# Four graph layers: counting the sources under layer 0's scatters, with the zeroing and the loads moved

## The reference, cut to what matters

```python
deg_n = segment_sum(ones, src); deg_e = segment_sum(ones, dst)
he  = Binv * segment_sum(x[src], dst)       # rows of edges into hyperedges (dst < 10000)
out = Dinv * segment_sum(he[dst], src) + b  # hyperedges back to the nodes
...
x = x + hconv(relu(hconv(h, W1)), W2)
```

## Time and profile before

| | us |
|---|---|
| median of 3 runs (3129.03 to 3147.51) | 3143.76 |
| the profiled execution | 3136.22 |
| its span | 3134.4 |

### The profile page before, as it was taken

How to read it: one execution, slowest core, us unless ns; L and a number is a source line. 1 busy time by engine, 2 the same in 40 slices (tenths; PEclk the granted TensorE clock), 3 DMA queues, 4 the chain that set the end, 5 groups by cost and what they waited for, 6 DMA issues and landing times. The chain is left out here.

```text
span 3134.4 us, 48304 instructions
## 1 busy us (share of the span) xinstructions
PE 2077.7 (66%) x10165; PEld 1475.8 (47%) x10165; DVE 2139.2 (68%) x8782; ACT 1682.8 (54%) x4590; POOL 1582.2 (50%) x1489
## 2 busy tenths in 40 slices
PE   3673534637767778788745788777776666664665
PEld 1332512525545656666632334343335655564555
DVE  5798523338877888898857777777745544444999
ACT  2592101238874656565647988898965444442222
POOL 3200565520007888888827666655607777774000
PEclk9896767879996677666767999999998888877999
DMA  2497422449997787787747999999966555554998
GB/s 72 146 360 304 80 56 75 101 114 323 322 306 264 243 249 230 244 255 234 235 103 216 290 290 286 283 294 286 292 170 216 178 186 181 181 175 137 316 316 280
DMA packets 494677, 696.59 MB, mean 222 GB/s; under 512 B 66363, under 2 KB 357398, under 8 KB 485932
## 3 DMA queue, kind: packets, MB, share of 16 engines
q1 hardware_dynamic: 416414, 511.30, 51.5%
q0 software_dynamic: 63360, 130.75, 15.6%
q10 hardware_dynamic: 14736, 52.96, 4.7%
HBM read 394.91 MB, written 327.18 MB: 230 GB/s over the span
## 5 line engine op out<-in xcount | busy, mean ns | idle before, releaser
L274 POOL DMA_INDIRECT xs<-x_d,table_src x400 | 386.7, 967 | 350.1 <-DVE x L1502 128.4
L274 POOL DMA_INDIRECT xs<-n_d,srcI x200 | 240.1, 1201 | 325.6 <-DVEq L1151 270.4
L274 POOL DMA_INDIRECT xd<-n_d,dstI x200 | 235.4, 1177 | 60.9 <-issue 54.5
L274 POOL DMA_INDIRECT xd<-x_d,table_dst x200 | 211.4, 1057 | 65.1 <-issue 64.5
L1860 PE MATMUL bank<-xs,same 128*128 128x129 f32 x400 | 109.2, 363 | 180.7 <-ACT sums L1829 93.0
L1721 POOL DMA_INDIRECT r_d<-rd,out_row x200 | 196.5, 982 | 60.9 <-issue 60.9
L1657 PEld LDWEIGHTS bank<-nmsg,same 128*128 128x128 f32 x400 | 61.4, 193 | 267.7 <-ACT sums L1589 209.0
L1657 PE MATMUL bank<-nmsg,same 128*128 128x128 f32 x400 | 99.9, 333 | 130.2 <-ACT sums L1589 74.9
L269 ACT ACTIVATE root<-tmp,eps 128x4 f32<-128x4 f32 (+3 forms) x253 | 76.8, 303 | 196.4 <-DVE tmp L245 195.8
L250 DVE RECIPROCAL rs<-root 128x4 f32<-128x4 f32 (+3 forms) x253 | 51.9, 205 | 185.5 <-ACT root L269 173.2
L474 POOL DMA_INDIRECT sum_d<-add,to x40 | 62.5, 1563 | 228.4 <-ACT add L663 187.7
(11 more groups left out here) (393 smaller groups left out, 7131.5 us busy)
## 6 DMA issues: line engine op xcount, KB each, us to landing
n_d<-T SPq DMA_DIRECT2D x98, 528.0 KB, 3.8
nt<-n_d SPq DMA_DIRECT2D x49, 1056.0 KB, 7.3
r<-r_d SPq DMA_DIRECT2D x98, 520.0 KB, 5.5
bc<-dst_d SPq DMA_DIRECT2D x170, 256.0 KB, 4.6
r_d<-nv SPq DMA_DIRECT2D x49, 528.0 KB, 7.7
v_d<-nv SPq DMA_DIRECT2D x49, 528.0 KB, 7.7
nv<-v_d SPq DMA_DIRECT2D x49, 528.0 KB, 4.3
x_d<-x SPq DMA_DIRECT2D x100, 256.0 KB, 4.8
```

Of the source, the lines that this page charges most:

```text
L274: pool.indirect_dma_start(out=out, out_offset=None, in_=table, in_offset=bass.IndirectOffsetOnAxis(ap=index, axis=0)).then_inc(s, 16)
```

## The change

The 52 source steps are placed differently: one in each group of the first gathers as before (now without the destinations, and behind the statistics), four in each group of the first scatters, and the rest, at least two, behind them. The destinations get steps of their own: three in each group of the second gathers, two in each of the second scatters, at least two behind. `hot` and `lows` shrink. `finalize` is cut in two: the source part (with a first store of `meta`) ends the first scatters, the destination part (with a second store) ends layer 0; parts of the other tables are made later too. The zeros come from padding rows of x within DRAM, 16 copies of 1.62 MB by ScalarE's queue right after the first loads. The loads are cut: 8 in `first_plan`, `K0` and ten and nine others by SyncE, ten by ScalarE; only the first 8 are waited for ahead of the columns. The two first gathers are issued ahead of the count of groups.

```diff
-            plan = [(rows...), ...]                     # 38 loads, all by SyncE
+            first_plan = [src, dst, next_dst, K, edge_weight, three columns of before]   # 8
+            plan = [...]                                # the other 29, and K0 by itself
+                    for dst, src in first_plan:
+                        sp.dma_start(dst, src, ...).then_inc(first_loads, 16)
+                    sp.dma_start(K0[:, :], ...).then_inc(k0_in, 16)
+                    for dst, src in plan[10:20]:
+                        sp.dma_start(dst, src, ...).then_inc(loads, 16)
                     sp.wait_ge(columns_in, 1)
                     for k, table in ((0, src_d), (1, dst_d)):
                         sp.dma_start(table..., rowsF[:, k, :, :]).then_inc(rows_out, 16)
+                    for dst, src in plan[20:]:
+                        sp.dma_start(dst, src, ...).then_inc(loads, 16)
...
+                    for dst, src in plan[0:10]:
+                        act.dma_start(dst, src, ...).then_inc(loads, 16)
+                    act.wait_ge(first_loads, 16 * len(first_plan))
+                    for k in range(16):
+                        act.dma_start(sum1_d[k * ZERO:(k + 1) * ZERO, :].rearrange("(p r) f -> p (r f)", p=96),
+                                      t["x"][N:N + ZERO, :].rearrange("(p r) f -> p (r f)", p=96)).then_inc(zeroed, 16)
                     act.wait_ge(weights_ps, 1)
...
-                            for k in range(NN // (P * 28)):
-                                sp.dma_start(sum1_d[...], zero_rows[:, 0:28 * D]).then_inc(zeroed, 16)
...
                     pe.wait_ge(columns_in, 1)
...
+                    pe.wait_ge(loads, 16 * len(plan))
+                    nc.tensor.transpose(bank[4][:, 0:D], wq[:, :], ident)
...
+                    def sources(k, b, of_low=False):        # TensorE
+                        pe.wait_ge(hot_ready, k + 1)
+                        pe.wait_ge(lows_ready, k + 1)
+                        for j in range(G): ...              # bank 0, of_low also bank 1
+                        last.then_inc(hot_used, 1)
+                    def destinations(k, b): ...             # bank 2, col_ready and col_used
...
                             last.then_inc(e["sums_ps"], 1)
+                            if conv == 1:
+                                for k in range(3):
+                                    destinations(g * 3 + k, (s + k) % 2)
                         bounded(pe, n, sums)
-                            bounded_from(pe, n, NH, histogram)
...
                             last.then_inc(e["he_ps"], 1)    # end of hyperedges
+                            if conv == 0:
+                                sources(n + g * 4, 0)
...
+                        def counted(g, s):
+                            for k in range(3 - conv):
+                                if conv == 0: sources(n + g * 4 + (k + 1), (k + 1) % 2)
+                                else:         destinations(n * 3 + g * 2 + k, k)
+                        lagged_thirds(pe, n, hyperedges, combined, counted)
+                        combined(n - 1, 1)
+                        m = steps_behind(pe)
+                        bounded(pe, m, behind)
...
+                            lagged_thirds(act, n, rows_of_edges, additions, signed)   # conv 0
+                            bounded(act, m, behind)
+                            additions(n - 1, 1)
...
+                            if conv == 0:                   # VectorE, reached, behind combine and later
+                                sources(n + g * 4, 0, n + g * 4)
                             dve.wait_ge(e["he_ps"], g + 3)
...                                                         # binv
+                            for k in range(3 - conv): ...   # sources or destinations
                             if conv == 0:
                                 dve.wait_ge(e["landed"], g + 1)
...                                                         # to
+                        bounded(dve, m, behind)
+                        of_sources(m) if conv == 0 else of_destinations(m)
...
+def lagged_thirds(eng, count, first, second, third):
+    first(0, 0); third(0, 0); first(1, 1); second(0, 0); third(1, 1)
+    with eng.Fori(2, count - 1, 2) as i:
+        first(i, 0); second(i - 1, 1); third(i, 0)
+        first(i + 1, 1); second(i, 0); third(i + 1, 1)
```

More of the change, by code:

```diff
@@ L43 @@
 COPY = 4096
+ZERO = 3168
 TW = 132
@@ L122, in lagged @@
     second(count - 1, 1)
+def lagged_thirds(eng, count, first, second, third):
+    first(0, 0)
+    third(0, 0)
+    first(1, 1)
+    second(0, 0)
+    third(1, 1)
+    with eng.Fori(2, count - 1, 2) as i:
+        first(i, 0)
+        second(i - 1, 1)
+        third(i, 0)
+        first(i + 1, 1)
+        second(i, 0)
+        third(i + 1, 1)
 def lagged_by_two(eng, count, first, second):
@@ L344, in build @@
                 "combine_ready", "comb_ps", "later_link", "to_ready", "add_ready", "added", "landed", "last_cols_ready",
-                "last_ps", "last_in")} for conv in range(2)]
+                "last_ps", "last_in", "counted")} for conv in range(2)]
             er_in, bc_in, sums_out, sums_back, bcd_in, bcs_in = (
@@ new lines, in sources @@
+                    def sources(k, b, at, of_low=False):
+                        dve.wait_ge(hot_used, k + 1)
+                        for j in range(G):
+                            for part, hi in enumerate(("hs", "hl") if of_low else ("hs",)):
+                                last = nc.vector.tensor_scalar(hot[:, b, j, part * NHI:(part + 1) * NHI], iota[:, 0:NHI],
+                                                               split[hi][:, bass.ds(at * G + j, 1)], None, ALU.is_equal)
+                        last.then_inc(hot_ready, 1)
@@ new lines, in destinations @@
+                    def destinations(k, b):
+                        dve.wait_ge(col_used, k + 1)
+                        for j in range(G):
+                            at = bass.ds(k * G + j, 1)
+                            nc.vector.tensor_scalar(hot[:, b, j, 0:NHI], iota[:, 0:NHI], split["hd"][:, at], None, ALU.is_equal)
+                            last = nc.vector.tensor_scalar(lows[:, b, j, :], iota[:, :], split["ld"][:, at], None, ALU.is_equal)
+                        last.then_inc(col_ready, 1)
@@ L928, in reached @@
                             nc.vector.reciprocal(binv[:, s, :], binv[:, s, :]).then_inc(e["binv_ready"], 1)
+                            for k in range(3 - conv):
+                                if conv == 0:
+                                    sources(n + g * 4 + (k + 1), (k + 1) % 2, n + g * 4 + (k + 1))
+                                else:
+                                    destinations(n * 3 + g * 2 + k, k)
                             if conv == 0:
```

324 lines of the change are left out of this document (186 added, 138 removed).

## The result

| | kernel before | changed kernel |
|---|---|---|
| median, us (range, 4 runs each) | 3145.29 (3129.03 to 3147.51) | 3198.15 (3196.93 to 3203.28) |
| profiled span, us | 3134.4 | 3196.0 |
| mean granted TensorE clock | 0.833 | 0.825 |

The ratio is 1.0184, 95% interval 1.0153 to 1.0215: slower, by 1.8%. The forecast was 3192 us. (The kernel before has one run more here than ahead of the prediction, so its median is 3145.29 and not 3143.76.) The span is read in three pieces. Up to the second gathers (`ix` on GpSimd) the changed kernel loses 33.8 us (448.12 against 414.32); from there to the start of the next block 31.4 us (287.0 against 255.6); the rest of the program is 3.6 us shorter. Sum 61.6, the difference of the spans.

A forecast was written before the change was run, and what follows sets the result against it. ScalarE's sign tables pace layer 0's counting, over full DMA engines. +38.5 us up to the second gathers and +12 after, on 3136.2, make 3187; 7.5 more for the median gives 3194, written 3192. Range 3065 to 3230.

The forecast's parts named there:

- Turns: Start of layer 0: queues alternate packet for packet, so loads wait out the zeroing and land at 104 us instead of 22.
- split of a turn: Zeroing time: 60 us for its bytes at 431 GB/s plus 48 shared turns at 0.66 us, 32 us; 88 taken.
- the low end of 60 us: Zeroing in layer 0: lowest time considered, 25.95 MB at the unshared 431 GB/s; the high end was 92.
- Rival A: Start of layer 0: a turn is many small packets, so loads land by 22 us; 3035 us in all, chance 0.2.
- First gathers: First gathers of layer 0: 6.65 us a group, the copy of x issued at 178.6 us instead of 136.4.
- Copy of x: Between first gathers and scatters: 89 us with nothing covering it, first combine at about 267 us, where it was 294.83.
- First scatters: First scatters with four counting steps a group: 16.2 us a group, 158 us for the stage, up 59.
- the ring: First scatters: additions, signs, counting, hyperedges and combined sums wait for each other in a circle, 16.2 us a group.
- Rival B: First scatters: contention as forecast, but ScalarE's 11.9 us a group sets the pace; 3152 us in all, chance 0.22.
- Behind them: From the last `to` of the first scatters to the second gathers: 27.8 us, 20.3 before.
- Second gathers and scatters: Added destination steps mostly hide under GpSimd's 11 us a group: +12 us, ends 0 and +27.
- 2.5 + 1.7 + 5.5 + 1 + 1.7: Second gathers: time of a group if the third destination step, waiting for TensorE's sums, closes late: 12.4 us.

The follow-up runs named there:

- e1: Changed kernel with the zeroing copies cut into 3 KB pieces instead of some 50 KB: 3457.41 us, one run, beside 3425.73 for the kernel before on that chip.
- e2: Changed kernel with the zeroing issued only once all loads have landed: 3487.93 us, one run, beside 3425.73 for the kernel before on that chip.
- e3: Changed kernel with the copy of x in 26 copies spread over the first scatters: 3402.18 us, one run, beside 3425.73 for the kernel before.
- e4: Changed kernel without the 40 source steps in the first scatters: 3425.85 us, one run, beside 3425.73 for the kernel before on that chip.
- e7: Changed kernel, first scatters with four table buffers, signs after the additions, counting one group late: 3501.69 us, one run, beside 3468.28 for the kernel before.
- e9: Changed kernel with e3's spread copy, e7's late count and a third destination buffer in the second gathers: 3085.93 us, ratio 0.9844 to the kernel before.
- e8: e9 with the zeroing behind all loads, partly spread over the first gathers, and smaller pieces in both copies: 3032.17 us, ratio 0.9668 to the kernel before.

## Why the prediction was right, and where it was off

The mechanism and nearly every landmark were right.

- **Turns.** First loads in and zeroing issued at 8.79 us (forecast 9). Packets one for one. Loads in with the end of the zeroing: first weight copy 100.57, h of group 0 ready at 109.8 (forecast 114.5). e1 shows that it is turns: smaller packets, same bytes, loads 53 us sooner. Not foreseen was that SyncE itself is held while it issues: 60.7 us at five 64 KB loads, 6.75 to 14.50 each, where e2, with no zeroing in the way, has 0.43 or 0.44 each. The loads came in with the end of the zeroing as forecast, so no cost of its own shows here; the same effect on ScalarE ate e1's gain. The forecast's split of a turn, the bytes at 431 GB/s and 0.66 us for the sharing, is not borne out: e1's zeroing alone ran at 332 GB/s. Its 88 us came close all the same, since it took the two parts together, which is the shared rate; the low end of 60 us rests on the 431 alone, which the copies within DRAM reach in no stretch shown here. Rival A, small loads passing the zeroing, is refuted.
- **First gathers.** 6.6 us a group, forecast 6.65; copy of x issued at 174.58, forecast 178.6.
- **Copy of x.** First combine 263.29, forecast 267. e3 shows that this stretch was bare: 74.5 us come back once the copy has cover.
- **First scatters.** 16.1 us a group, forecast 16.2; last `to` at 420.7, forecast 425. e4 and e7 show the ring. Rival B, ScalarE's 11.9 us, did not happen in the change; e7 makes it happen, at 11.7, by its order of work.
- **Behind them.** 27.4 us to the second gathers, forecast 27.8 (the terms written there, 8.5, 12.1 and 6.5, make 27.1). Up to there +33.8 against +38.5.
- **Second gathers and scatters: the mis-sized term.** +12 was forecast, with ends of 0 and +27; +31.4 was measured, beyond the high end. One of the forecast's own signs fails with it: the second gathers were to stay GpSimd's, and they are paced by the ring. The chain "2.5 + 1.7 + 5.5 + 1 + 1.7" was the right ring, but the sums were taken at 5.5 or 3.7 us where they take 5.4 in the first group and up to 6.7 in the later ones, and only 0.7 us a group was booked, where the chain with 5.5 already stands 1.4 over the 11 of GpSimd. With 6.5 the same chain gives 13.4, and the groups take 12.6 to 13.8, 13.4 in the mean, 2.3 over the 11.07 before, +20.6 in nine. e9 confirms it: with a third buffer 11.5 us. The rest, about 10 us, lies between the last h and the first scatter (34.0 us, before 29.2) and from the first to the last indirect DMA of the second scatters (107.9, before 103.0), where the forecast put the added destination steps at nothing. e8 has 33.8 and 106.8 there, so the third buffer doesn't touch it, and its cause stays open.
- **Sum.** The two errors, -4.7 and +19.4, and the later layers' -3.6 make +11.1 us: 3187 forecast for the profiled execution, 3197.78 measured. That the median lies only 6 us over the forecast is in part luck: 7.5 us were added to come from the profiled execution to the median, where the changed kernel's median lies 0.4 above its profiled one, and 2 us were taken off in writing 3192 for 3194.

## What to carry to other kernels

Work on the compute engines and transfers that overlap in one stretch are each other's cover; before moving the one, work out what the other takes alone, and where it will stand. A bulk copy in the same time as small loads costs them one of its packets per turn, so place it by turns and packet size, in doses, not by bytes alone. When work is put into a loop with two buffers, write the ring of waits through all engines and sum it at the slowest durations the rows show for that stage.

## What the hardware showed that was not expected

- A turn lasts by packet size: 0.22 us at 3 KB, 0.56 at 11 KB, 1.80 at some 50 KB pieces, one packet of the other queue in each. These are means over the pieces and the marks, the short packet that ends a copy on each engine.
- Copies from DRAM to DRAM moved 332 GB/s in 3 KB pieces with the engines to themselves (e1), and 320 to 331 in large pieces beside small loads (the changed kernel), where stores from SBUF alone moved 431.
- An engine can be held while it issues, for long when many packets stand in its queue or when its packets wait for another queue's large ones: 16 copies took ScalarE 10.34 us to issue in 50 KB pieces (3 packets per engine and copy, the mark included), 46.12 in 11 KB pieces (10) and 78.88 in 3 KB pieces (34), and SyncE up to 14.50 us for one 64 KB load beside the 50 KB pieces.
- TensorE's granted clock was 0.51, so nearly all at the lower level of 1.2 GHz, in the stretch where it idled under the copy of x, and 0.76 in the scatters behind it. In e3 and e8, which lack that idle stretch, the scatters had 0.78 and 0.77: the idling is not what holds the clock down there.
